# Head sums two units behind the cosines, tail sums three, in a GNN layer with cosine attention

## The reference

```python
h = relu(layernorm(x))
deg = clip(adj.sum(axis=1), 1.0); dis = deg ** -0.5
diffusion = (dis[:, None] * adj * dis[None, :]) @ h - h
norms = maximum(norm(h, axis=-1), 1e-8)
sim = h @ h.T / (norms[:, None] * norms[None, :])
attn = softmax(beta * sim * adj, axis=1)
out = x + diffusion + sigmoid(alpha) * (attn @ h - h)
```

## Time and profile before

| | us |
|---|---|
| median of 3 runs | 1859.82 (1858.98 to 1860.15) |
| the profiled execution | 1860.17 |
| its span, first to last instruction | 1858.0 |
| TensorE busy | 1829.2 |
| ScalarE busy | 1272.6 |
| VectorE busy | 1248.4 |
| GpSimd busy | 1210.4 |

### The profile page before, as it was taken

One profiled execution on the slowest core, in us unless ns is written; L12 is line 12 of the kernel. 1 busy time (PEld: TensorE's weight loads), 2 busy tenths in 40 slices (PEclk: granted clock), 3 DMA queues, 4 the chain that ended last, 5 costly groups with the idle time before them and its releaser, 6 DMA issues.

```text
span 1858.0 us, 44815 instructions
## 1 busy us (share of the span) xinstructions
PE 1829.2 (98%) x19632; PEld 1455.9 (78%) x19632; DVE 1248.4 (67%) x1537; ACT 1272.6 (68%) x1203; POOL 1210.4 (65%) x665
## 2 busy tenths in 40 slices
PE   5999999999999999999999999999999999999999
PEld 4777777777777777777777777777778888888888
DVE  7999999888997778778777877777775211011111
ACT  5989998888888899989998999898886000000000
POOL 3989898889888888888888888888872000000000
PEclk9999999999999999999999999999999999999999
DMA  9967777779877787776677877877337644545520
GB/s 150 190 92 108 110 115 99 96 98 119 116 100 100 107 102 104 105 103 93 92 103 96 100 100 108 101 109 97 112 108 283 224 167 166 190 171 186 200 103 12
DMA packets 188377, 229.39 MB, mean 123 GB/s; under 512 B 5908, under 2 KB 161556, under 8 KB 184084
## 3 DMA queue, kind: packets, MB, share of 16 engines
q0 software_dynamic: 133120, 67.12, 45.5%
q1 hardware_dynamic: 29380, 145.77, 21.4%
q10 hardware_dynamic: 25680, 13.63, 2.7%
HBM read 352.32 MB, written 75.50 MB: 230 GB/s over the span
## 4 chain that ended last, share of the span: by engine, by line
PE 96%; DVE 2%; ACT 1%; issue 1%; DMA 0%; POOL 0%; SPq 0%; DVEq 0%; ACTq 0%
PE cos_ps L847 34%; PE cos_ps L934 12%; PE top_ps L893 12%; PE top_ps L901 12%; PE top_ps L895 12%; PE top_ps L934 12%; DVE xe L718 1%; ACT xe L436 0%; PE cos_ps L908 0%; ACT ustage L432 0%; DMA asb<-x_in 0%; PE cos_ps L823 0%; ACT asb L381 0%; PE top_ps L913 0%; DVE ptmp L522 0%
## 5 line engine op out<-in xcount | busy, mean ns | idle before, releaser
L339 POOL TENSOR_TENSOR ustage<-xe,ustage 128x1024 f16<-128x1024 f32 x512 | 1096.1, 2143 | 175.4 <-ACT xe L436 167.0
L718 DVE TENSOR_TENSOR xe<-cos_ps,arena 128x1024 f32<-128x1024 f32 x512 | 626.5, 1224 | 220.4 <-PE cos_ps L847 133.4
L432 ACT ACTIVATE ustage<-xe,ebias,ab 128x1024 f16<-128x1024 f32 x512 | 635.2, 1241 | 130.7 <-DVE xe L718 129.3
L436 ACT ACTIVATE xe<-xe,ebias,ab 128x1024 f32<-128x1024 f32 x512 | 628.8, 1228 | 0.1
L893 PE MATMUL top_ps<-h,ustage 128*128 128x129 f16 x4096 | 516.0, 220 | 1.2 <-ACT asb L420 0.7
L895 PE MATMUL top_ps<-hlo,ustage 128*128 128x128 f16 x4096 | 515.3, 219 | 0.0
L895 PEld LDWEIGHTS top_ps<-hlo,ustage 128*128 128x128 f16 x4096 | 400.8, 98 | 58.6
L893 PEld LDWEIGHTS top_ps<-h,ustage 128*128 128x128 f16 x4096 | 400.7, 98 | 56.6 <-ACT asb L420 3.8
L901 PE MATMUL top_ps<-h,ustage 128*128 128x129 f16 x4096 | 315.8, 220 | 1.4 <-POOL ustage L339 1.4
L654 DVE TENSOR_REDUCE top_ps<-arena 128x8 f32<-128x1024 uint16 x256 | 311.6, 1217 | 0.0
L847 PE MATMUL cos_ps<-uT_hi 128*128 128x512 f16 x1024 | 304.8, 379 | 0.7 <-DVE xe L718 0.6
(11 more groups left out here) (116 smaller groups left out, 1047.9 us busy)
## 6 DMA issues: line engine op xcount, KB each, us to landing
arena<-adj_in_dram POOLq DMA_DIRECT2D x128, 512.0 KB, 10.7
at_scratch<-arena SPq DMA_DIRECT2D x128, 512.0 KB, 5.3
arena<-at_scratch SPq DMA_DIRECT2D x26, 2048.0 KB, 7.9
xe<-at_scratch SPq DMA_DIRECT2D x6, 2048.0 KB, 7.9
h_scratch<-asb SPq DMA_DIRECT2D x16, 256.0 KB, 10.9
arena<-h_scratch SPq DMA_DIRECT2D x16, 256.0 KB, 6.0
ustage<-h_scratch ACTq DMA_DIRECT2D x8, 512.0 KB, 4.1
ptmp<-x_in ACTq DMA_DIRECT2D x8, 512.0 KB, 5.5
```

Source lines behind the costliest of these rows:

```text
L339: nc.gpsimd.tensor_tensor(elo[:, n % ES, :], ef[:, n % XS, :], ehi[:, n % ES, :], ALU.subtract).then_inc(elo_done, 1)
L432: nc.scalar.activation(ehi[:, n % ES, :], xm[:, n % XS, :], ACT.Exp, bias=ebias[:, 0:1], scale=ab[:, 1:2]).then_inc(ehi_done, 1)
L436: nc.scalar.activation(ef[:, n % XS, :], xm[:, n % XS, :], ACT.Exp, bias=ebias[:, 0:1], scale=ab[:, 1:2]).then_inc(ef_done, 1)
L718: nc.vector.tensor_tensor(xm[:, n % XS, :], cos_ps[:, slot_of(n), :], at8[:, m % W, :, n % B], ALU.mult).then_inc(x_done, 1)
```

## The change

`sums` is cut into two functions. `heads(n)` holds the waits at a run's start and the sixteen head matmuls, `tails(n)` the rest. The loop now issues, in step n: cosines(n), heads(n-2), tails(n-3). Where n-2 is the first unit of a run other than the first, its heads are left out of that step and issued at the front of the next one, behind the cosines and ahead of the next unit's heads; so there step m is cosines(m), tails(m-3), and step m+1 is cosines(m+1), heads(m-2), heads(m-1), tails(m-2). The waits stay what they were, and so do the programs of the other engines and `LAG`, by which they place `copy_acc` and `add_acc`. `degrees()` and `degrees_to_tiles()` keep their steps and come behind that step's head sums.

```diff
--- before.py
+++ after.py
@@ -39,6 +39,7 @@
     HB = TILES // 8
     READY = 2
     WARM = 24
+    HEAD_LAG = 2
     LAG = 3
     RS = 3
     EIGHT = 56
@@ -63,6 +64,9 @@
     DONE = [[((0, 1), False), ((2, 3), True), ((4, 5), False), ((6, 7), True)],
             [((0, 1), False), ((2, 3), True), ((4, 5), True), ((6,), False), ((7,), True)]]
     STORES = [[(0, 4), (4, 8)], [(0, 4), (4, 6), (6, 8)]]
+
+    def new_run(n):
+        return n > 0 and n % 16 == 0 and n < UNITS and RUN_OF[n // 16] != RUN_OF[n // 16 - 1]
 
     def slot_of(n):
         return (n + sum(1 for m in AHEAD if m <= n)) % 2
@@ -867,23 +871,20 @@
                                             start=(b == 0), stop=True, skip_group_check=True)
                 last.then_inc(deg_moved, 1)
 
-            def sums(n):
+            def place_of(n):
                 run = RUN_OF[n // 16]
                 panel, k0, k1 = RUNS[run]
-                s = 16 * ORDER[n // 16][1] + n % 16
-                first, final = n == 16 * k0, n == 16 * k1 - 1
+                return run, panel, 16 * ORDER[n // 16][1] + n % 16, n == 16 * k0, n == 16 * k1 - 1
+
+            def heads(n):
+
+                run, panel, s, first, _ = place_of(n)
                 if first and 0 < run <= ADDED[0]:
                     pe.wait_ge(acc_copied, run)
                 elif first and run and run - 1 in ADDED:
                     pe.wait_ge(acc_added, run - len(ADDED))
                 elif first and run:
                     pe.wait_ge(acc_copied, run - len(ADDED))
-                if n == UNITS - 11:
-                    degrees()
-                if n == UNITS - 9:
-                    degrees_to_tiles()
-
-
                 pe.wait_ge(ehi_done, n + 1)
                 if panel < 3 and n % 4 == 0:
                     pe.wait_ge(hlo_ready, s // 4 + 1)
@@ -894,6 +895,13 @@
                                      start=(first and t % 3 == 0), stop=False, skip_group_check=True)
                     nc.tensor.matmul(top_ps[:, bank, col:col + P], head, hlo[:, s, :],
                                      start=False, stop=False, skip_group_check=True)
+
+            def tails(n):
+                run, panel, s, _, final = place_of(n)
+                if n == UNITS - 11:
+                    degrees()
+                if n == UNITS - 9:
+                    degrees_to_tiles()
                 pe.wait_ge(elo_done, n + 1)
                 for t in range(PT):
                     bank, col = t // 3, t % 3 * HS
@@ -917,8 +925,13 @@
                         pe.wait_ge(x_done, n - 1)
                         transposed(AHEAD[n], (slot_of(n) + 1) % 2)
                     cosines(n)
+
+                if new_run(n - HEAD_LAG - 1):
+                    heads(n - HEAD_LAG - 1)
+                if HEAD_LAG <= n < UNITS + HEAD_LAG and not new_run(n - HEAD_LAG):
+                    heads(n - HEAD_LAG)
                 if n >= LAG:
-                    sums(n - LAG)
+                    tails(n - LAG)
 
             for k in range(CHUNKS):
                 panel, ch = k // CH, k % CH
```

## The result

The changed kernel takes **1868.14 us** (median of 6 runs, 1867.44 to 1868.75) against 1859.8 us of the kernel before (6 runs); the ratio is 1.0045, 95% interval 1.0034 to 1.0056. So it is slower, as forecast, by 8.3 us where 6.4 were forecast. The profiled execution took 1868.22 us with a span of 1866.1 us, 8.1 more than before.

A forecast was written before the change was run, and what follows sets the result against it. TensorE, a gapless stream of matmuls except at run changes, was taken as the bound; 6.65 us at the changes less 0.3 for mask waits, other terms 0, gave +6.4 us, median 1866.2 us, range 1863.4 to 1869.2.

The forecast's parts named there:

- Inside a run: Steps between run changes: heads move one 2.65 us step earlier, nothing waits and nothing is won; 500 steps cost 0.
- The first units: Loop start: early heads fill gaps, unit 3 begins 0.2 us later, later cosines come at the same times; 0 with the end.
- The run changes: Ten run changes: TensorE asks for the banks 0.90 us earlier, but their readers mostly do not follow; 6.65 us in all.
- d: Time by which a bank's reader starts earlier at a run change; 0 to 0.40 us, mean 0.23.
- The two mask waits behind unit 16: Two TensorE waits of some 0.15 us for masks behind unit 16 should vanish, VectorE being late there; -0.3 us.
- `degrees()`: It comes 0.9 us later inside its step; clip_deg on VectorE may wait some tenths, hidden by the masks' cover; 0.
- The end: Before the last tails: three head blocks instead of four, so the wait for GpSimd grows by 0.90 us, the time does not.
- Rival 3: TensorE's clock falls to half after each new wait, 2.65 us more each, ten times 26.5, so 1892.7 us; chance 2%.
- The sum: Whole kernel: run-change costs of 6.65 us less 0.3 for mask waits, +6.4 us; bounds +4.5 to +9.0.
- Rival 1: At run changes copies and additions begin 0.90 us earlier too, nothing is lost: -0.3 us, 1859.5; chance 12%.

The follow-up runs named there:

- changes_given_back: Changed kernel with heads three units behind, not two, for each run's last two units and the next run's first; 1863.70 us, 1.0019 of the kernel before.
- readers_first: Changed kernel with ScalarE's copies put ahead of the fp32 exponential and VectorE's additions ahead of the mask at run changes; 1859.42 us, 0.9999 of the kernel before.

## Why the prediction was right, and what it missed

- **Inside a run: 0.** Right. In changes_given_back the heads keep their two units of distance almost everywhere, and between changes the cosines keep their distance to those of the kernel before.
- **The first units: 0.** Right, to 0.02 us for unit 4; unit 3 is 0.2 us late as worked out.
- **The run changes: 0.90 less d.** Right for each of the ten to 0.04 us, from one row each for the place of the reader. readers_first raises d to 0.9 without touching TensorE's order and the whole cost goes.
- **The two mask waits behind unit 16, -0.3.** Wrong: both are still there with 0.16 us each. They were misread. The cosines wait there not for a mask but for VectorE's copy of transposed rows (L624, now L628), and VectorE had itself waited for TensorE's transposes before it (in the kernel after):

```profile
99.01 1.23 DVE L627 CAST uT_hi<-cos_ps 128x1024 f16<-128x1024 f32 x1 [0.16 <-PE cos_ps L827]
...
101.55 0.15 PEld L851 LDWEIGHTS cos_ps<-uT_hi 128*128 128x128 f16 x2 [0.17 <-DVE uT_lo L628]
```

A wait that begins with TensorE's own work moves back with TensorE and can't absorb its delay.

- **`degrees()`: 0.** 0.11 us, small but not nothing: the prediction priced a wait of VectorE for it and not its new place on TensorE.
- **The end: "the wait grows by 0.90 us, the time does not".** This is the step that failed. The arithmetic of the wait was nearly right (1.81 us idle for 1.11, 0.7 more and not 0.9; the last heads wait for their exponential and take the rest), but the time behind it grew by 1.5 us in the execution shown, where the clock fell. The forecast weighed a fall at the ten changes, gave it 2%, called 1.7 us at unit 16 the longest new wait although its own wait at the end came to 2, and put no price on it there. Rival 3 came true once instead of ten times.
- **The sum.** The loop grew by 6.54 us where 6.4 were forecast, and part of that closeness is luck: the missing -0.3 and the 0.11 of the degrees were offset by costs at the changes 0.2 below forecast. Without the fall the changed kernel stands at about 1865.9, with it at 1867.4 to 1868.8, so the median of 1868.14 lies in the upper part of the range for a reason that the forecast didn't have.
- **Rival 1** (the readers follow the tails) fell: the copies at unit 256 follow the exponential by 1.13 us, where 1.14 was forecast from unit 80.

## What to carry to other kernels

When producer work is pulled ahead, ask at each hand-over what stands in front of the consumer in its own program; if that has not moved, the hand-over doesn't move either, and the producer only comes to wait earlier. One row, the instruction ahead of the consumer and what ended the idle time between them, gives the price to a few hundredths of a microsecond. Before you count a wait as slack that will absorb a delay, follow it back one step: if it begins with the delayed engine's own work, it moves along. A wait of TensorE that was made longer may cost more than its own length, so look at the granted clock behind it in more than one execution.

## What the runs showed of the hardware

The clock's fall behind a wait of 1.8 us is a matter of the single execution: by its mean clock the same kernel had it in five of six executions at one time and in one of five at another. Behind a wait of 1.1 us it came in none of 128 executions, behind one of 1.8 us in 16 of 51, and it cost 1.5 and 1.7 us in the two profiles that have it. With sixteen small matmuls in that wait, none of whose results is used, the kernel took 2.0 us less than the kernel after where that one's clock mostly fell, and as long as it (1866.17 against 1865.95) where it mostly did not. What decides whether it falls stays open.
